# Moving VectorE's preparation and statistics between stages of a patch-transformer tower, and twelve filler products on TensorE

## What is computed

```python
h = gelu(unfold(x, 64x25, stride 12) @ weight + bias)        # 128 x 82 x 64
h = h + relu_attention(layernorm(h))    # relu(q k^T), masked, divided by the row number
h = h + moe6(layernorm(h))              # router of 2 layers, top 2 of 6, experts of 3 layers
h = h + rope_attention(layernorm(h))    # softmax, causal, rotary part of 16 columns
h = h + moe8(layernorm(h))              # router of 1 layer, top 2 of 8, gelu experts of 2 layers
```

## Time and profile before

| what | value |
|---|---|
| runs | 638.49, 646.17, 647.04 us; median 646.17 us |
| profiled execution, its own time | 641.96 us |
| its span, first to last instruction | 640.2 us |
| mean granted clock of TensorE | 0.971 |
| TensorE busy | 582.6 us (91%) |
| VectorE busy | 502.4 us (78%) |
| ScalarE busy | 307.3 us (48%) |
| GpSimd busy | 149.1 us (23%) |
| chain that ended last | PE 70%, DVE 17%, issue 5%, ACT 4%, DMA 2% |

### The profile page before, as it was taken

The page is one execution under the profiler, slowest core; times in us unless marked ns, Lnnn a source line. Parts: engine busy times, 40 slices in busy tenths (PEclk is TensorE's granted clock), DMA queues, the critical chain, the costliest instruction groups (busy, mean ns, idle before and its releaser), DMA issues.

```text
span 640.2 us, 17643 instructions
## 1 busy us (share of the span) xinstructions
PE 582.6 (91%) x6943; PEld 369.7 (58%) x6943; DVE 502.4 (78%) x1503; ACT 307.3 (48%) x738; POOL 149.1 (23%) x151
## 2 busy tenths in 40 slices
PE   0999999979999899999998989999997899999993
PEld 0895565548987544454444357777775445455441
DVE  3657788996785879878878547988987999998863
ACT  0020000004343476777776638687873456555651
POOL 1000000854448104105000351505350222121000
PEclk9999999989999999999999999999995899999998
DMA  8998667210000000000000000000000000001111
GB/s 294 412 388 322 259 234 253 47 20 2 2 2 2 2 2 2 2 2 2 3 1 2 1 1 2 3 2 2 2 2 0 3 22 22 20 20 23 23 24 29
DMA packets 28899, 39.21 MB, mean 61 GB/s; under 512 B 19984, under 2 KB 20368, under 8 KB 28816
## 3 DMA queue, kind: packets, MB, share of 16 engines
q1 hardware_dynamic: 27016, 36.87, 16.6%
q10 hardware_dynamic: 1800, 1.20, 0.8%
HBM read 35.37 MB, written 2.69 MB: 59 GB/s over the span
## 4 chain that ended last, share of the span: by engine, by line
PE 70%; DVE 17%; issue 5%; ACT 4%; DMA 2%; POOL 0%; SPq 0%; DVEq 0%; ACTq 0%; POOLq 0%
PE bank L415 15%; PE bank L1584 8%; PE bank L1620 5%; PE bank L1622 4%; DVE m_hm L1881 3%; PE bank L1071 3%; PE bank L1645 3%; PE bank L1594 3%; PE bank L1021 3%; PE bank L1035 2%; PE bank L1605 2%; PE bank L814 2%; PE bank L1573 2%; PE bank L1029 2%; PE bank L800 2%
## 5 line engine op out<-in xcount | busy, mean ns | idle before, releaser
L581 POOL TENSOR_TENSOR centred<-h,mean 82x512 f32<-82x512 f32 x64 | 72.9, 1139 | 424.1 <-DVE rstd L564 293.3
L415 PE MATMUL bank<-cols,tok_weight 64*64 64x328 f32 (+1 forms) x1800 | 116.6, 415 | 15.8 <-DVE cols L459 14.5
L1457 ACT ACTIVATE m_h<-bank,m_b 128x656 f32<-128x656 f32 x112 | 90.3, 807 | 79.7 <-PE bank L1584 79.2
L1881 DVE TENSOR_TENSOR m_hm<-bank,m_h 128x656 f32<-128x656 f32 x112 | 94.0, 840 | 30.6 <-PE bank L1594 27.3
L415 PEld LDWEIGHTS bank<-cols,tok_weight 64*64 64x64 f32 x1800 | 76.9, 138 | 51.1 <-issue 17.9
L1584 PE MATMUL bank<-m_xt,m_w 64*64 64x328 f32 x896 | 89.7, 471 | 1.2 <-ACT m_h L1457 1.2
L458 DVE COPY cols<-image 128x1992 f32<-128x1992 f32 x32 | 62.1, 1953 | 16.8 <-DMA image<-in_x_dram 14.5
L1620 PE MATMUL bank<-m_hm,m_wo 64*64 64x328 f32 x512 | 48.4, 447 | 3.0 <-DVE m_osb L1888 2.3
L980 ACT ACTIVATE sa_prob<-sa_masked,sa_low 82x82 f32<-82x82 f32 x128 | 44.6, 350 | 12.5 <-DVE sa_low L1125 12.5
L392 ACT ACTIVATE tok_fm<-bank,tok_bias 128x328 f32<-128x328 f32 x16 | 7.7, 530 | 86.1 <-PE bank L415 86.1
L1464 ACT ACTIVATE m_h<-bank,m_b 128x328 f32<-128x328 f32 x96 | 45.7, 527 | 2.2 <-PE bank L1605 2.2
(11 more groups left out here) (184 smaller groups left out, 1047.6 us busy)
## 6 DMA issues: line engine op xcount, KB each, us to landing
image<-in_x_dram SPq DMA_DIRECT2D x32, 1000.0 KB, 10.6
out_dram<-m_fin SPq DMA_DIRECT2D x16, 164.0 KB
tok_weight<-in_L_tok_weight_dram ACTq DMA_DIRECT2D x2, 400.0 KB, 7.9
m_w<-in_L_ffn_w_dram SPq DMA_DIRECT2D x2, 128.0 KB
m_sel_raw<-c_sel_dram SPq DMA_DIRECT2D x1, 256.0 KB
m_w<-in_L_ffn_expert_w_dram SPq DMA_DIRECT2D x2, 96.0 KB
m_wo<-in_L_ffn_expert_w_dram SPq DMA_DIRECT2D x4, 48.0 KB
m_sel_raw<-c_sel_dram SPq DMA_DIRECT2D x1, 192.0 KB
```

What stands on the lines that cost most here:

```text
L415: return pe.matmul(sum_bank[u % 2][s][t * D:(t + 1) * D, L * j0:L * j1], weight[s * R:(s + 1) * R, c, :], cols[u % 2][s * R:(s + 1) * R, c ...
L581: pool.tensor_tensor(self.centred[:], slots(self.h, g), mean.broadcast_to([L, G, D]), ALU.subtract).then_inc(self.shifted, 1)
L1457: act.activation(h1[n % RING][:], h1_bank, ACT.Gelu if last else ACT.Relu, bias=W.b1[:, k:k + 1]).then_inc(h1_ready, 1)
L1881: dve.tensor_tensor(hm[k][:], cb_bank, src[n % RING][:], ALU.mult).then_inc(hm_ready, 1)
```

## The change

It has five parts.

1. `prepare` of M leaves P. It goes to R, in the steps of groups 10, 11 and 12. ScalarE and TensorE wait at a mixture's start for its loads only; TensorE waits for `prepared` at the first spread.
2. `ends` of `ln1` and `ln3` become (6, 10, 16). In R, `ln0`'s last part goes one step earlier, `ln1`'s first part goes from groups 8 to 10 to groups 7 to 9, and `ln1`'s second part is new in R, at groups 12 to 14. M does the rest of `ln1`, then both the first and second part of `ln2`. S does `ln2`'s last part (one piece a step), then two parts of `ln3`.
3. In N, the 14 instructions of `ln3`'s second part leave the gaps in front of `weigh` (0, 2) and (0, 3). Three of the four sets of statistics leave the front: they stand behind `weigh` (0, 3), (1, 2) and (2, 1). The routing of the first pair, its bf16 split included, goes in front of S's last residual addition.
4. The turn of group 4 in N is written to bank 4 and waits for the last copy of the probabilities instead of for `scaled`. ScalarE copies group 3's turn before the last probabilities, and group 4's after the first expert output. TensorE waits for `scaled` in front of the first `turn_combine`.
5. `keep_busy(n)` issues n bf16 products of 128 rows and 512 columns into bank 7, which nothing reads: 4 behind the turn of group 14's probabilities, 3 behind the turn of group 4, 5 in front of the first `turn_combine`.

VectorE has as many instructions as before, at other places and some on other widths; TensorE gets 12 more.

```diff
-            norm.append(LayerNorm(sem, f"ln{i}", shared, xn[i % 2], i % 2 == 0, norm[-1] if i else None, (7 if i == 1 else NG // 2, 3 * NG // 4, NG)))
+            norm.append(LayerNorm(sem, f"ln{i}", shared, xn[i % 2], i % 2 == 0, norm[-1] if i else None, (6, 10, NG) if i % 2 else (NG // 2, 3 * NG // 4, NG)))
...
@@ build, scalar: the last three turns of S and N @@
-                    go(s, 2)
+                    go(s, 2 if f < 2 else 1)
@@ build, vector @@
-                go(s, 2)
+                go(s, 1)
+                go(n, 1)
+                go(s, 1)
@@ stage_patches, vector @@
-            if u == NU - 2:
-                go(moe[0].prepare(dve))
@@ stage_relu_attention, vector @@
-            if 2 <= g <= 7:
+            if 1 <= g <= 6:
                 go(scale_mine, 1)
-            if 8 <= g <= 10:
+            if 7 <= g <= 9:
                 go(scale_next, 2)
+            if 10 <= g <= 12:
+                go(prepare, 2 if g == 11 else 1)
+            if 12 <= g <= 14:
+                go(scale_more, 2)
@@ stage_rope_attention, vector @@
-            if 1 <= g <= 3:
-                go(scale_mine, 2)
-            if 4 <= g <= 7:
-                go(scale_last, 2 if g < 6 else 1)
-            if 9 <= g <= 11:
+            if 1 <= g <= 6:
+                go(scale_mine, 1)
+            if 7 <= g <= 9:
                 go(scale_next, 2)
+            if 11 <= g <= 13:
+                go(scale_more, 2)
@@ stage_moe, tables of N, then of M @@
-        SCALE_MINE, SCALE_NEXT = ({(0, 2): 3, (0, 3): 3}, {(1, 1): 1, (2, 3): 1, (3, 1): 1, (4, 3): 1, (5, 1): 1, (6, 3): 1}), ()
-        COUNT, PREPARE = {}, ()
+        SCALE_MINE, SCALE_NEXT = ({}, {(2, 3): 1, (3, 0): 1, (3, 2): 1, (4, 1): 1, (4, 3): 1, (5, 0): 1}), ()
+        COUNT, PREPARE = {(0, 3): NG - 3, (1, 2): NG - 2, (2, 1): NG - 1}, ()
...
-        SCALE_MINE = {(1, 0): 2, (1, 1): 1, (1, 2): 3}, {(3, 0): 2, (5, 0): 2, (7, 0): 2}
+        SCALE_MINE = {}, {(1, 0): 1, (1, 1): 1, (1, 2): 1, (3, 0): 1, (3, 2): 1, (4, 2): 1}
@@ stage_moe, tensor @@
-        return psum[:, (0, 2, 3, 2, 0)[f], :] if last and f <= FRONT else front
+        return psum[:, (0, 2, 3, 2, 4)[f], :] if last and f <= FRONT else front
...
+                elif f == FRONT:
+                    pe.wait_ge(before.p_ready, NG)
...
+        def keep_busy(n):
+            pe.wait_ge(before.biased, NG)
+            for _ in range(n):
+                pe.matmul(psum[:, 7, :], ident16[:], W.sel[:], start=True, stop=True)
...
+            keep_busy(4)
...
             turn(FRONT)
+            keep_busy(3)
...
+                    keep_busy(5)
+                    pe.wait_ge(before.scaled, NG)
                     pe.wait_ge(x_ready, FRONT + 1)
                     pe.wait_ge(before.biased, NG)
                     turn_combine(0)
@@ stage_moe, vector, front of N @@
-            count(NG - 4)
+            yield
             take_logits(2)
-            yield
             route_last(0, 3)
             route_last(0, 4)
-            count(NG - 3)
             take_logits(3)
-            route_last(0, 5)
-            count(NG - 2)
-            yield
-            for r in range(6, 9):
+            for r in range(5, 9):
                 route_last(0, r)
-            count(NG - 1)
+            yield
+            count(NG - 4)
```

More of the change, by code:

```diff
@@ L183, in build @@
         Z = zeroed_tiles(sb, sem)
-        R = stage_relu_attention(nc, ctx, sem, psum, h, stats, ident, attn, norm[0], norm[1], Z, P)
+        R = stage_relu_attention(nc, ctx, sem, psum, h, stats, ident, attn, norm[0], norm[1], Z, P, moe[0])
         with ExitStack() as inner:
@@ L693, in rope_weights, with stage_relu_attention @@
     return W
-def stage_relu_attention(nc, stack, new_sem, psum, h, stats, ident, weights, mine, following, Z, before):
+def stage_relu_attention(nc, stack, new_sem, psum, h, stats, ident, weights, mine, following, Z, before, later):
     def sb(name, shape, dt=F32):
@@ L849, in vector @@
     def vector(dve):
-        scale_mine, scale_next = mine.scale(dve, 2), following.scale(dve, 0)
+        scale_mine, scale_next, scale_more = mine.scale(dve, 2), following.scale(dve, 0), following.scale(dve, 1)
+        prepare = later.prepare(dve)
         for i, t in enumerate(pt):
@@ L1147, in statistics @@
             ins.then_inc(following.counted, 1)
-        scale_mine, scale_last, scale_next = mine.scale(dve, 1), mine.scale(dve, 2), following.scale(dve, 0)
+        scale_mine, scale_next, scale_more = mine.scale(dve, 2), following.scale(dve, 0), following.scale(dve, 1)
         rope_parts(0)
@@ L1180, in stage_rope_attention @@
     S.gpsimd, S.scalar, S.tensor, S.vector = gpsimd, scalar, tensor, vector
-    S.qk_ready, S.v_ready, S.biased, S.scaled, S.added = qk_ready, v_ready, biased, scaled, added
+    S.qk_ready, S.v_ready, S.biased, S.scaled, S.added, S.p_ready = qk_ready, v_ready, biased, scaled, added, p_ready
     return S
@@ L1309, in stage_moe @@
         COMBINE, SECOND = 2, (0, 1)
-        SCALE_MINE = {(1, 0): 2, (1, 1): 1, (1, 2): 3}, {(3, 0): 2, (5, 0): 2, (7, 0): 2}
-        SCALE_NEXT = {(11, 0): 2, (11, 2): 1, (13, 0): 2, (13, 2): 1}, {}
-        PREPARE = ((5, 2), (7, 2), (9, 0), (9, 2))
+        SCALE_MINE = {}, {(1, 0): 1, (1, 1): 1, (1, 2): 1, (3, 0): 1, (3, 2): 1, (4, 2): 1}
+        SCALE_NEXT = ({(10, 2): 1, (11, 0): 1, (11, 2): 1, (12, 2): 1, (13, 0): 1, (13, 2): 1},
+                      {(14, 0): 1, (14, 1): 1, (14, 2): 2, (15, 0): 2})
+        PREPARE = ((5, 2), (7, 0), (7, 2), (9, 0))
         COUNT = {(0, LAST): NG - 1}
@@ L1470, in output @@
             act.activation(osb[:], o_bank[:, 0:HALF], ACT.Copy).then_inc(o_ready, 1)
-        act.wait_ge(prepared, W.n_prepared)
+        act.wait_ge(W.loaded, W.n_loads * 16)
         if last:
@@ L1478, in scalar @@
             act.activation(unused[:], W.first[:, 0:1], ACT.Gelu)
-            copy_x(FRONT)
         else:
@@ L1490, in scalar @@
         hidden1(0, 0)
+        if last:
+            copy_x(FRONT)
         for g in range(NG):
@@ L1531, in turn @@
             if last and f <= FRONT:
-                if f in (0, FRONT):
-                    pe.wait_ge(before.scaled, NG if f else NG - 4)
+                if f == 0:
+                    pe.wait_ge(before.scaled, NG - 4)
+                elif f == FRONT:
+                    pe.wait_ge(before.p_ready, NG)
                 elif f < 3:
@@ L1588, in spread @@
             n = g * NP + k
+            if n == 0:
+                pe.wait_ge(prepared, W.n_prepared)
             pe.wait_ge(c_ready, g + 1)
```

4 lines of the change are left out of this document (2 added, 2 removed).

## The result

The changed kernel takes 636.6 us (median of four runs, 634.8 to 639.6), the kernel before, run beside it, 645.7 (638.5 to 647.0). The ratio is 0.990, with a 95% interval of 0.985 to 0.995: faster by about 1%, which is inside the 2% of "no change" that the prediction named. The forecast was 630.7, a gain of 2.4%; 636.6 lies inside the range of 623 to 640. The profiled execution took 639.63 us, its span is 637.8 us; before they were 641.96 and 640.2. So a gain of 13.3 us was forecast from one profile to the other, and these two profiles differ by 2.3.

What follows compares the result with a forecast made beforehand. TensorE was taken to bound the kernel, except where it stands still or runs slowly. 5.4 + 1.8 - 1.7 + 0.5 + 7.3 = 13.3 off the profiled 641.96 gives 628.7; the median was set 2 above, 630.7, range 623 to 640.

Steps and rivals of the forecast that it cites:

- P, 5.4: End of P: without `prepare`, TensorE's 3.66 us pause and the low clock behind it (1.75) go; gain 5.4 us.
- `ln1`'s first part a step earlier, 1.8: R: TensorE's 1.78 us wait for POOL's first normalised group of M goes; gain 1.8 us.
- 24 more instructions in R, -1.7: R's steps 10 to 14: VectorE's added instructions are partly hidden; loss 1.7 us, bounds 0.8 and 5.
- the work moved into R costs more than it should: Rival, R's last steps: nine small VectorE instructions stretch beside POOL, 4 us more; 633.7 us, chance 0.10.
- The forecast's own sign of being wrong: The clock line still has a 5, or VectorE's rows at R's end show many of about 1 us.
- M and S, 0.5: M and S: small instructions move between places; gain 0.5 us, bounds -2 and +3.
- N, 7.3: Front of N: 6.4 + 1.7 - 0.8, a gain of 7.3 us, bounds 5 and 9.
- the 6.4 to `weigh` (0, 0): Front of N: with the clock up, VectorE's 9.2 us queue sets the time; `weigh` (0, 0) starts 6.4 us earlier.
- (c): N, `weigh` (0, 0) to (1, 0): 14 scale instructions go, one set of statistics comes in; 1.7 us less.
- (d): N's groups 1 and 2: two other sets of statistics, less scale instructions leaving group 1; loss 0.8 us.
- the clock falls all the same: Rival, front of N: the clock is lost despite the products, leaving about 1 of N's 7.3; 635.0 us, chance 0.20.
- the slower case: Rival: the clock is lost at M's head and N's front and stays down; 644.6 us, chance 0.04.

Runs made afterwards that it cites:

- e4: The kernel before with one edit, `prepare` moved from the end of P to R's steps 2 to 5; 639.9 us, ratio 0.992.
- e6: The changed kernel with `prepare` in P behind unit 5's statistics and `ln1`'s second part in M's groups 0 and 1; 627.7 us, ratio 0.976.
- e5: The changed kernel with `prepare` in P behind unit 5's statistics instead of R's steps 10 to 12; 632.0 us, ratio 0.981.
- e12: The changed kernel once more, unedited, with a second profile; 637.1 us, ratio 0.990.
- e7: e5 with the copy of N's third logits moved in front of S's residual of group 14; 631.0 us, ratio 0.9795.
- e10: e9 without the 12 filler products; 627.3 us, ratio 0.974.
- e9: The changed kernel with the edits of e5, e6 and e7 together; 627.2 us, ratio 0.974.
- e3: The changed kernel without its 12 filler products; 637.1 us, ratio 0.990.

## Why the prediction was wrong

Point by point, the forecast's terms against the profiles:

- *P, 5.4.* Right: 5.35 in the changed kernel, 5.2 in e4. It was not given back by a wait at R's first groups.
- *`ln1`'s first part a step earlier, 1.8.* Right: no TensorE row of M's first turn waits for POOL any more, and R without the moved parts (e6) is 2.1 us shorter than before.
- *24 more instructions in R, -1.7.* This is the step that failed, and in it the sentence "groups 10 to 13 hide theirs, partly". The 24 cost R's masks 9.6 us (71.1 against e6's 61.6), beyond even the upper bound of 5. The sum counted the extra work of steps 13 and 14 only and took 0.2 us for each instruction. I had written beside it that such instructions stretch with POOL at work, but did not carry it to `prepare`: with the first part of `ln1` one step earlier, POOL normalises with hardly a gap from 183 to 195 us, R's steps 10 and 11, just where `prepare` was put. Six of its instructions in step 11 took 4.35 us, in a place where VectorE in e5, without them, waits 0.77 for the next mask's scores. The copy of M's logits, queued behind them, made TensorE wait 2.6, and the wait cost the clock. `prepare` cost 6 to 7 us in R where nothing was counted; the scale pieces 2.4, where 1.7 was: step 12 1.6, step 13 0.1, step 14 1.0 (e5 against e6; 0.3 were gained ahead of them), of which I had 0, 0.8 and 1.0. In e5's step 12 two of them stretch as well (L549 0.95 and L551 0.96 us), since POOL there works until 196.56.
- *The rival "the work moved into R costs more than it should"* was this mechanism, and went by 4 us and 0.10. It took the nine instructions of steps 13 and 14 as the ones that stretch; these took 0.2 each (one 0.47), because POOL was done by then. What it missed is `prepare`, and who is queued behind the stretched ones. The forecast's own sign of being wrong, VectorE rows of about 1 us near R's end, came true: four, in step 11.
- *M's head.* I counted 1 us there, and only in a rival. It lost 3.1 in one profile of the changed kernel and 0.4 in the other. e5 against e6 puts 1.0 to the scale pieces. The rest goes with the clock: its mean over the 18 us around M's head is 0.72 where the head takes 23.7 us (215 to 233) and 0.91 where it takes 21.0 (e12, 213 to 231).
- *M and S, 0.5.* Measured 0.2.
- *N, 7.3.* 8.2, but by another split. Of the 6.4 to `weigh` (0, 0) came 4.8. VectorE's queue took 9.5 us (485.76 to 495.29) where I had 9.2, but my check of TensorE began at `cp`: it left out that TensorE needs the third logits' copy, which stands behind the residual in that queue, and VectorE waited 1.21 for TensorE at the end. In e7 the front is 6.35 shorter than before, as forecast. All these are against one profile of the kernel before, whose front was 1.8 us longer than e4's; against e4 the changed kernel's gain in N is 6.3, not 8.2, so that N came out near its forecast is in part luck. (c), 1.7, came out at 1.5. (d), a loss of 0.8, was a gain of 1.9; why, no run here separates.
- *The rival "the clock falls all the same"* came true in its event and not in its price. It did fall, behind the 1.43, and N still gained 8.2. I had priced a low clock at 6.3; e10 against e9 measures about 10 us more of it at 0.6 to 0.7. The products, which were to hold it, are worth 0.4 us in e3 and 0.5 in e10, from S's last mask to the end. I had also taken the fall in the kernel before to follow from its pause of 0.98 us; e4 has the same pause and kept the clock.

Two slips of the working change nothing that was forecast. If all four spread products ran side by side, the rows would give 0.53 us for one of 512 columns, not half of 0.27; measured are about 0.22. And in the slower case, 8.6 less what 3.4 us at the low level lose by the same ratio (1.5) is 7.1, not 6.6.

The sum was reachable: e6 ends 14.0 us before the kernel before, and its ratio of 0.976 is that of the forecast. It needs `prepare` and the scale pieces taken out of R. The Trainium skill's rule on long gaps (TensorE: Matmul & The Clock Gate, "HAM oscillation — how this bites in real kernels") was set against the rows in the prediction. By it no wait here would lose the clock; in these runs too it fell behind waits of 1.43 to 2.61 us.

What stays open: which of the reorderings at N's front (VectorE's counts, ScalarE's copy, the bank) is worth how much. They were not tried apart, except the place of the third logits' copy (e7). Nor does a run tell the clock's share of R's loss from the stretching's; the 4.0 and 3.1 above are read from two profiles.
